# Two more row tiles transposed by DMA in a sandwich layer on eight cores

## The chip, the cores and the metric

The kernel runs on all eight cores of one Trainium2 chip. Each core takes half the rows of one of four batches (2048 of 4096 rows) and needs nothing from the others. The metric is the device time of the slowest core in microseconds. A core has TensorE for matmuls, VectorE (DVE), ScalarE (ACT), GpSimd (POOL), and a sync engine (SP) that issues DMAs. DMAs issued by GpSimd go through queue q0 (software), those issued by SP through queue q1 (hardware), and both are carried out by the same 16 DMA engines.

## The reference

```
def _L0_attn_ref(x, W_qkv, W_out):
    B, S, H = (8, 2048, 1024)
    scale = 1.0 / np.sqrt(h).astype(np.float32)
    y = jnp.einsum('bsh,oh->bso', x, W_qkv).reshape(*x.shape, 3)
    q, k, v = (y[..., 0], y[..., 1], y[..., 2])
    scores = jnp.einsum('bqh,bkh->bqk', q, k) * scale
    attn = jax.nn.softmax(scores, axis=-1)
    ctx = jnp.einsum('bqk,bkh->bqh', attn, v)
    return jnp.einsum('bsh,oh->bso', ctx, W_out)
...
x = x + _layernorm(_L0_attn_ref(_layernorm(x), W_qkv, W_out))
x = x + _layernorm(_L0_ffn_ref(_layernorm(x), router_w, w1, b1, w2, b2))
```

x has the shape (4, 4096, 1024). The feed-forward part is two matmuls with 4096 hidden units and a gelu between them, scaled by the sum of a router's two normalised weights. All matmuls run in bfloat16 with sums in float32.

## The kernel before, in words

A core holds the normalised rows of its whole batch in on-chip memory: 32 tiles of 128 rows (`xn`), of which tiles 0 to 15 are its own query rows (from `xo`) and 16 to 31 the other half (from `xr`). They are also needed transposed (`xnT`), with the 1024 features on the partitions, as the keys and as the operand from which q' is made.

The work up to the first scores goes like this:

- **The product of the query and key weights** (`am`, bfloat16, L116 `wkb,wqb`), so that the scores are x am x'.
- **q' in four groups of four row tiles** (`g` = 0 to 3). A group has eight blocks (`j`), one for each 128 output features; a block is eight matmuls of 512 columns (four tiles of 128 rows) that add up in one PSUM bank (`q_part`), and a copy by ScalarE to `qst` (`q_out`, L466). The banks rotate over six (`next_free`). Group 0 is cut up finely since its tiles come in late. `store_q` writes a group to memory, and `load_q` reads single tiles (`qt`) back; `store_q(0)`, `load_q(0)` and `load_q(1)` come ahead of groups 2 and 3 in the program.
- **The product of the value and output weights** (`bm`, L116 `wob,wvb`), 128 matmuls.
- **The scores, the softmax and the context** for 16 query tiles, and then the feed-forward part.

Each row tile is loaded by GpSimd's queue with a cast to bfloat16 (`fetch_x`). All tiles from 16 on are asked for in one go once `am` is done, behind the value and output weights (`wvb`, `wob`). VectorE takes a tile's statistics (`stats_x`), ScalarE forms the reciprocal of the deviation (`rsa`), and VectorE normalises the tile in place (`apply_x`, L294). From tile 12 on two tiles go together.

A tile is then transposed in one of two ways, and the constant `NTP` says in which. Below `NTP` it is `transpose_x`: eight 128x128 transposes on TensorE (L120) into bank 6 or 7 and a copy by ScalarE into `xnT` (L327). From `NTP` on `apply_x` itself issues one DMA transpose on the sync queue (L112), right behind the normalisation:

```
            if t >= NTP:
                t_xT[t] = DT(keys(t), xt, [t_ln[t]])
```

Every engine runs its instructions in the order in which the program puts them. The program is written out by hand in that order: a call of `norm_next` or `transpose_x` between two blocks fixes the place. Waits are on semaphores; the first matmul of a `q_part` waits for the transposed tiles that it reads and, where it opens a bank, for the copy that frees it. SP's semaphores are a ring of 16, so a DMA also waits for the one 16 issues earlier.

Of the kernel before, what the change touches and what calls it, by code (L numbers as in the profile page):

```python
# [14 lines left out]
HC = 8  # L15
# [4 lines left out]
NKT = 32  # L20
FF = 4096
NFC = 32
NTP = 16

ENGINES = ("sync", "gpsimd", "vector", "scalar", "tensor")
SEM_OF = {"vector": "vS", "scalar": "sS", "tensor": "tS", "gpsimd": "gS"}
# [53 lines left out]
def build_program():  # L80
# [33 lines left out]
    def MM(o, l, m, first, last, after=(), sig=False):  # L114
        return Q.put("tensor", lambda e, o=o, l=l, m=m, f=first, s=last:
                     e.matmul(o, l, m, start=f, stop=s), after, sig)  # L116
# [131 lines left out]
    def keys(t):  # L248

        return xnT[:, t * H:(t + 1) * H].rearrange("p (c k) -> p c k", c=HC)  # L250

    def keys4(t, c, n=4):

        return xnT[:, t * H:(t + n) * H].rearrange(
            "p (t c k) -> p c t k", t=n, c=HC)[:, c]
# [32 lines left out]
    def apply_x(u):  # L288
# [3 lines left out]
        for t in units[u]:  # L292
# [3 lines left out]
                [a])  # L296
            if t >= NTP:
                t_xT[t] = DT(keys(t), xt, [t_ln[t]])
# [5 lines left out]
    def norm_apply():  # L304
        if applied[0] < units_done[0]:
            apply_x(applied[0])
            applied[0] += 1

    def norm_next():
        u = units_done[0]  # L310
        stats_x(u)
        if applied[0] < u:
            norm_apply()
        units_done[0] += 1
# [4 lines left out]
    def transpose_x(t):  # L319
        b = 6 + t % 2  # L320
        for j in range(HC):
            tok = TP(tbank[b][:, j * 128:(j + 1) * 128],
                     xn[:, t * H + j * 128:t * H + (j + 1) * 128],
                     [t_ln[t], t_id, free[b]] if j == 0 else (), j == HC - 1)
        dst = keys(t)
        src = tbank[b].rearrange("p (c t) -> p c t", c=HC)
        t_xT[t] = free[b] = A(lambda e: e.copy(dst, src), [tok])  # L327
# [104 lines left out]
    def load_q(i):  # L432
        t_qt[i] = DS(qt[i % 2][:, :], qs[i],
                     [t_qs[i], t_s.get((i - 2, 3))])
# [5 lines left out]
    def next_free():  # L440
        b = rot[0] % 6
        rot[0] += 1
        return b

    def q_part(g, j, b, t0, n):

        for i in range(HC):
            aft = []
            if i == 0:
                aft = t_xT[4 * g + t0:4 * g + t0 + n]  # L450
                if t0 == 0:
                    aft.append(free[b])
            if g == 0 and t0 == 0 and j % 4 == 0:
                aft.append(t_am[j // 4][i])
            tok = MM(bank[b][:, t0 * 128:(t0 + n) * 128],
                     am[:, i * H + j * 128:i * H + (j + 1) * 128],
                     keys4(4 * g + t0, i, n),
                     i == 0, i == HC - 1, aft, i == HC - 1)
        return tok

    def q_out(g, j, b, tok, toks):
        o = qst[g % 3][:, :].rearrange("p (k j t) -> p k j t", k=4,
                                       j=HC)[:, :, j]
        s = bank[b].rearrange("p (k t) -> p k t", k=4)
        war = t_qs[4 * (g - 3)] if g >= 3 else None
        free[b] = A(lambda e: e.copy(o, s), [tok, war])  # L466
        toks.append(free[b])
# [3 lines left out]
    def store_q(g):  # L471
        d = DS(qs[4 * g:4 * g + 4].rearrange("k p f -> p k f"),
               qst[g % 3][:, :].rearrange("p (k f) -> p k f", k=4), t_qo[g])
        for k in range(4):
            t_qs[4 * g + k] = d
# [20 lines left out]
    for g in range(NQG):  # L496
        toks = []
        if g == 0:
            first = [(4, 0), (5, 1), (6, 3), (7, 2), (0, 4), (1, 5)]
            for j, b in first[:2]:  # L500
                q_part(0, j, b, 0, 1)
            transpose_x(1)
            for j, b in first[2:4]:
                q_part(0, j, b, 0, 1)
            norm_next()
            norm_next()
            norm_apply()
            for j, b in first[:4]:
                q_part(0, j, b, 1, 1)
            q_part(0, 0, 4, 0, 2)  # L510
            transpose_x(2)
            q_part(0, 1, 5, 0, 2)
            transpose_x(3)
            norm_next()
            for j, b in first:
                q_part(0, j, b, 2, 1)
            norm_next()
            done = []
            for n, (j, b) in enumerate(first):
                done.append((j, b, q_part(0, j, b, 3, 1)))  # L520
                if n == 1:
                    q_out(0, *done[0], toks)
                    q_out(0, *done[1], toks)
                    norm_next()
                    transpose_x(4)
            norm_next()
            transpose_x(5)
            for d in done[2:4]:
                q_out(0, *d, toks)
            done.append((2, 0, q_part(0, 2, 0, 0, 4)))  # L530
            transpose_x(6)
            norm_next()
            q_part(0, 3, 1, 0, 2)
            transpose_x(7)
            done.append((3, 1, q_part(0, 3, 1, 2, 2)))
            for d in done[4:]:
                q_out(0, *d, toks)
            norm_next()
            rot[0] = 2
        if g == 2:  # L540
            norm_apply()
        for j in range(HC if g else 0):
            if j in norm_at.get(g, ()):
                norm_next()
            b = next_free()
            q_out(g, j, b, q_part(g, j, b, 0, 4), toks)
            if g < 3 and j in (0, 2, 4, 6):
                transpose_x(4 * (g + 1) + j // 2)
        t_qo.append(toks)
        if g == 0:  # L550
            store_q(0)
        if g == 1:
            load_q(0)
            load_q(1)
# [575 lines left out]
```

How the kernel before makes its waits and increments, by code:

```python
            def body(e, items=self.items[eng]):  # L66
                seen = {}
                for after, fn, name, inc in items:
                    for s, v in after:
                        if v > seen.get(s, 0):
                            e.wait_ge(sems[s], v)
                            seen[s] = v
                    ins = fn(e)
                    if name is not None:
                        ins.then_inc(sems[name], inc)
```

## Time and profile before

| | us |
|---|---|
| median of 3 runs (1086.77 to 1164.91) | 1087.37 |
| the profiled execution | 1087.49 |
| its span on the slowest core (core 5) | 1085.9 |
| spans of the eight cores | 1084.3 to 1085.9 |
| mean granted TensorE clock | 0.997 to 0.998 |
| TensorE busy | 1064.1 (98%) |
| VectorE, ScalarE, GpSimd busy | 350.4, 315.1, 101.9 |

The span goes from the first to the last instruction; the time of an execution is 1.6 us more. All times below are counted from the start of the span of core 5. The run at 1164.91 lies apart from the other two. Busy times of different engines overlap, so they don't add up.

### The profile page before, as it was taken

The page shows a single profiled execution, that of the slowest core. Times are in us where ns is not written, and L with a number is a line of the kernel's source. Part 1 is how long each engine was busy: PE and PEld are TensorE (multiplying, and loading weights), DVE is VectorE, ACT ScalarE, POOL GpSimd, SP SyncE. Part 2 cuts the span into 40 slices and gives each one's busy share as a digit, 9 for nine tenths or more (in the row PEclk, how much of TensorE's full clock was granted, in tenths as well). Part 3 has the DMA queues.
Part 4 walks back from the last instruction along what each step waited for, and adds up shares of the span by engine and source line. Part 5 has one row for each costly group of instructions (what it writes and reads, how often), then busy time and mean ns, then how long its engine had stood idle before and what let it go on. Part 6 is the DMA issues. An engine that isn't in the chain of part 4 may idle for free.

```text
span 1085.9 us, 14321 instructions; the slowest of 8 cores (1084.3 to 1085.9 us)
## 1 busy us (share of the span) xinstructions
PE 1064.1 (98%) x5288; PEld 495.7 (46%) x5288; DVE 350.4 (32%) x723; ACT 315.1 (29%) x516; POOL 101.9 (9%) x175
## 2 busy tenths in 40 slices
PE   5999999999999999999999999999999999999996
PEld 2654444444444444444444444444444444444444
DVE  0673842333433333334332322006103300330033
ACT  1474432323332223233322323203520242023300
POOL 7430000000000000000000320001000000000000
PEclk9999999999999999999999999999999999999999
DMA  8999994443244444433349999985202220220012
GB/s 121 161 183 172 173 225 85 107 101 83 80 78 96 98 107 107 98 83 80 80 88 150 166 165 195 162 161 115 80 1 78 75 43 1 70 73 13 1 46 71
DMA packets 154980, 110.57 MB, mean 102 GB/s; under 512 B 119712, under 2 KB 130208, under 8 KB 154912
## 3 DMA queue, kind: packets, MB, share of 16 engines
q0 software_dynamic: 31120, 62.94, 29.4%
q1 hardware_dynamic: 123792, 46.72, 22.1%
q8 instruction: 43, 0.70, 0.3%
q14 instruction: 25, 0.20, 0.1%
HBM read 88.69 MB, written 25.17 MB: 105 GB/s over the span
## 4 chain that ended last, share of the span: by engine, by line
PE 94%; DMA 2%; DVE 1%; POOL 1%; issue 1%; ACT 1%; POOLq 0%; DVEq 0%; ACTq 0%
PE pAll L116 94%; DMA xn<-xo 2%; POOL wkb L110 1%; PE pAll L120 0%; POOL wqb L110 0%; ACT xnT L327 0%; DVE st L277 0%; DVE st L279 0%; DVE am L389 0%; ACT qst L466 0%; DVE yt L978 0%; ACT rsa L284 0%; DVE nma L290 0%; POOLq L1079 0%; DVE xn L294 0%
## 5 line engine op out<-in xcount | busy, mean ns | idle before, releaser
L116 PE MATMUL pAll<-xnT,qt 128*128 128x512 bf16 x1024 | 225.1, 379 | 0.0
L116 PE MATMUL pAll<-xn,pT 128*128 128x512 bf16 x1024 | 223.6, 379 | 0.0
L116 PE MATMUL pAll<-x2T,w1b 128*128 128x512 bf16 x1024 | 222.6, 379 | 0.0
L116 PEld LDWEIGHTS pAll<-xnT,qt 128*128 128x128 bf16 x1024 | 100.2, 98 | 120.8 <-issue 0.5
L116 PEld LDWEIGHTS pAll<-xn,pT 128*128 128x128 bf16 x1024 | 100.2, 98 | 120.8
L116 PEld LDWEIGHTS pAll<-x2T,w1b 128*128 128x128 bf16 x1024 | 99.8, 98 | 120.0 <-issue 0.6
L597 DVE TENSOR_REDUCE nmx<-pAll 128x1 f32<-128x1024 f32 x64 | 78.0, 1222 | 177.0 <-PE pAll L116 177.0
L603 ACT ACTIVATE pb<-pAll,nmx 128x1024 bf16<-128x1024 f32 x64 | 71.3, 1114 | 167.6 <-DVE nmx L597 167.5
L116 PE MATMUL pAll<-w2b,h1a 128*128 128x512 bf16 (+1 forms) x528 | 113.2, 373 | 0.2 <-issue 0.2
L116 PE MATMUL pAll<-w2b,h1b 128*128 128x512 bf16 (+1 forms) x528 | 113.0, 373 | 0.0
L974 ACT ACTIVATE x2r<-x2r,nm 128x1024 f32<-128x1024 f32 x15 | 17.2, 1147 | 214.4 <-DVE nm L972 214.4
L116 PEld LDWEIGHTS pAll<-w2b,h1a 128*128 128x128 bf16 x528 | 51.6, 98 | 59.5 <-issue 0.6
L116 PEld LDWEIGHTS pAll<-w2b,h1b 128*128 128x128 bf16 x528 | 51.6, 98 | 58.9
L945 DVE TENSOR_TENSOR yt<-pAll,b2b 128x1024 f32<-128x1024 f32 (+2 forms) x18 | 19.9, 1104 | 180.7 <-PE pAll L116 180.7
L841 ACT ACTIVATE h1b<-pAll,b1f 128x512 bf16<-128x512 f32 x64 | 43.2, 687 | 60.0 <-PE pAll L116 59.9
L116 PE MATMUL pAll<-xnT,am 128*128 128x512 bf16 (+2 forms) x392 | 58.5, 305 | 0.7 <-ACT xnT L327 0.7
L116 PE MATMUL pAll<-bm,uT 128*128 128x512 bf16 x256 | 57.9, 379 | 0.0
L841 ACT ACTIVATE h1a<-pAll,b1f 128x512 bf16<-128x512 f32 x64 | 42.8, 685 | 50.1 <-PE pAll L116 50.1
L658 ACT CAST ub<-pAll 128x1024 bf16<-128x1024 f32 x16 | 16.2, 1012 | 119.5 <-PE pAll L116 119.5
L116 PE MATMUL pAll<-wkb,wqb 128*128 128x512 bf16 x128 | 30.0, 394 | 12.2 <-DMA wkb<-wk 12.0
L116 PEld LDWEIGHTS pAll<-xnT,am 128*128 128x128 bf16 x392 | 31.2, 98 | 22.9 <-issue 1.1
L110 POOL DMA_DIRECT2D x2s<-xf x16 | 8.7, 545 | 345.6 <-DVE xf L719 345.6
(91 smaller groups left out, 601.1 us busy)
## 6 DMA issues: line engine op xcount, KB each, us to landing
xf<-xo POOLq DMA_DIRECT2D x16, 512.0 KB, 4.6
x2s<-xf POOLq DMA_DIRECT2D x16, 512.0 KB, 2.9
w1b<-w POOLq DMA_DIRECT2D x8, 1024.0 KB, 22.4
w2b<-w POOLq DMA_DIRECT2D x8, 1024.0 KB, 60.1
x2r<-x2s POOLq DMA_DIRECT2D x16, 512.0 KB, 4.7
y<-yt SPq DMA_DIRECT2D x15, 512.0 KB, 2.7
xn<-xo POOLq DMA_DIRECT2D x16, 256.0 KB, 30.4
xn<-xr POOLq DMA_DIRECT2D x16, 256.0 KB, 49.7
```

The costliest lines, as they stand in the source:

```text
L110: "gpsimd", lambda e, o=o, i=i: e.dma_start(o, i), after)
L116: e.matmul(o, l, m, start=f, stop=s), after, sig)
L597: mx = V(lambda e: e.tensor_reduce(n, pair[pr], AX, ALU.max, negate=True), [tok, t_cf.get(i - 2)])
L603: lambda e: e.activation(o, pair[pr], AF.Exp, bias=n, accum_out=l),
L658: t_ub[i] = A(lambda e: e.copy(o, pair[2]), [t_ctx[i], t_uT.get(i - 2), t_qs[NQT - 1]])
L841: lambda e: e.activation(o, bank[b], AF.Gelu_apprx_tanh, bias=b1f[:, fc:fc + 1]),
L945: a = V(lambda e, c=c, acc=acc: e.tensor_tensor(o[:, c], acc, b2b[:, c], ALU.add), [done, t_b2] + war)
L974: a = A(lambda e: e.activation(x[:, :], x[:, :], AF.Identity, bias=n_), [t_n, t_x2r[t]])
```

## The change

`NTP` goes from 16 to 14: tiles 14 and 15 are no longer transposed on TensorE but by DMA. Group 3 of q' reads tiles 12 to 15. Its first three blocks are formed in two halves: first the columns of tiles 12 and 13 for all three, in three banks, then those of tiles 14 and 15. The other five blocks stay whole.

```
-NTP = 16
+NTP = 14
...
         if g == 2:
             norm_apply()
-        for j in range(HC if g else 0):
+        if g == 3:
+            three = [next_free() for j in range(3)]
+            for j, b in enumerate(three):
+                q_part(g, j, b, 0, 2)
+            for j, b in enumerate(three):
+                q_out(g, j, b, q_part(g, j, b, 2, 2), toks)
+        for j in range({0: HC, 3: 3}.get(g, 0), HC):
             if j in norm_at.get(g, ()):
                 norm_next()
             b = next_free()
             q_out(g, j, b, q_part(g, j, b, 0, 4), toks)
-            if g < 3 and j in (0, 2, 4, 6):
+            if g < 3 and j in (0, 2, 4, 6) and 4 * g + 4 + j // 2 < NTP:
                 transpose_x(4 * (g + 1) + j // 2)
```

On TensorE, from the middle of group 2 to the end of group 3 (`xnT,am` are blocks of q', `ident,xn` the transposes of a tile, `wob,wvb` the product that follows):

```order
 L116 MATMUL pAll<-xnT,am 128x512 x16
 L120 MATMUL pAll<-ident,xn 128x128 x8
-L116 MATMUL pAll<-xnT,am 128x512 x16
-L120 MATMUL pAll<-ident,xn 128x128 x8
-L116 MATMUL pAll<-xnT,am 128x512 x16
-L120 MATMUL pAll<-ident,xn 128x128 x8
-L116 MATMUL pAll<-xnT,am 128x512 x72
+L116 MATMUL pAll<-xnT,am 128x512 x40
+L116 MATMUL pAll<-xnT,am 128x256 x48
+L116 MATMUL pAll<-xnT,am 128x512 x40
 L116 MATMUL pAll<-wob,wvb 128x512 x128
```

Two groups of eight transposes are gone, and 24 matmuls of 512 columns have become 48 of 256.

On the sync queue, from the two loads of `qt` to the stores of the other groups:

```order
 L108 DMA qt_69<-qs 128x1024
 L108 DMA qt_70<-qs 128x1024
-L112 DMA_TRANSPOSE xnT<-xn 128x8x128 x16
+L112 DMA_TRANSPOSE xnT<-xn 128x8x128 x18
 L108 DMA qs<-qst_53 128x4x1024
 L108 DMA qs<-qst_54 128x4x1024
```

The two new transposes stand directly behind the loads of `qt` and ahead of the 16 of the other half's tiles.

## Rows read from the trace of the kernel before

**Rows 1.** The page: busy time and share of the span; the chain that ended last.

```profile
PE 1064.1 (98%) x5288; PEld 495.7 (46%) x5288; DVE 350.4 (32%) x723; ACT 315.1 (29%) x516; POOL 101.9 (9%) x175
...
PE 94%; DMA 2%; DVE 1%; POOL 1%; issue 1%; ACT 1%; POOLq 0%; DVEq 0%; ACTq 0%
```

**Rows 2.** Timeline of TensorE: start, length, operation, count.

```profile
49.16 1.04 PE L116 MATMUL pAll<-xnT,am 128*128 128x256 bf16 x8
50.03 0.61 PE L120 MATMUL pAll<-ident,xn 128*128 128x128 bf16 x8
...
90.93 0.61 PE L120 MATMUL pAll<-ident,xn 128*128 128x128 bf16 x8
91.37 15.70 PE L116 MATMUL pAll<-xnT,am 128*128 128x512 bf16 x72
106.91 5.34 PE L116 MATMUL pAll<-wob,wvb 128*128 128x512 bf16 x24
```

**Rows 3.** Timelines of VectorE and ScalarE: tiles 14 and 15 normalised, tile 15 copied.

```profile
77.94 1.00 DVE L294 TENSOR_SCALAR xn<-xn,rsa,nma 128x1024 bf16<-128x1024 bf16 x2
...
91.66 1.02 ACT L327 COPY xnT<-pAll 128x1024 bf16<-128x1024 bf16 x1
```

**Rows 4.** Timelines of the two queues: loads of qt, last load of the other half.

```profile
79.12 0.95 SPq L108 DMA_DIRECT2D qt<-qs  x2
...
62.35 0.53 POOL L110 DMA_DIRECT2D xn<-xr  x1 [0.72 <-DMA xn<-xo]
```

**Rows 5.** Tile xnT from 104 to 109 on SP (issue in ns); page, all 16.

```profile
L112 SPq DMA_TRANSPOSE xnT<-xn x2: 1798/5278/8758, 105.8 to 107.7; - x2
...
DMA to landing us min/median/max: 13.3/13.8/14.3
...
xnT<-xn SPq DMA_TRANSPOSE x16, 4.0
```

**Rows 6.** Stretches: length, busy PE, PEld, DVE, ACT, POOL; clock, DMA share, GB/s.

```profile
90.00:104.00 14.00, 14.00 (x73) 6.62 (x71) 5.87 (x12) 5.34 (x10) 0.00 (x0) 1.00 1.07 165
104.00:114.00 10.00, 10.00 (x48) 4.51 (x46) 7.67 (x17) 4.42 (x12) 0.00 (x0) 1.00 1.08 173
```

**Rows 7.** DMA queues (packets, MB, share) in 79:90, 84:88, 110:113, 120:121.

```profile
q1 hardware_dynamic: 288, 0.52, 17.7%
...
q0 software_dynamic: 203, 0.39, 73.9%
q1 hardware_dynamic: 202, 0.38, 36.3%
...
q0 software_dynamic: 241, 0.44, 96.6%
q1 hardware_dynamic: 198, 0.05, 12.2%
...
q1 hardware_dynamic: 1136, 0.28, 128.0%
```

**Rows 8.** DMA queues 638 to 653, and the transpose issued at 636.8, w2 loading.

```profile
q1 hardware_dynamic: 1056, 0.26, 17.6%
...
uT<-ub SPq DMA_TRANSPOSE x1, 15.1
```

**Rows 9.** TensorE's first and last matmuls, then stretches as in rows 6.

```profile
9.62 7.10 PE L116 MATMUL pAll<-wkb,wqb 128*128 128x512 bf16 x24 [9.62 <-DMA wkb<-wk]
...
1075.72 1.91 PE L116 MATMUL pAll<-w2b,h1b 128*128 128x256 bf16 x16
...
1080.00:1082.00 2.00, 0.00 (x0) 0.00 (x0) 1.67 (x5) 0.00 (x0) 0.20 (x1) 0.82 0.00 0
1082.00:1084.00 2.00, 0.00 (x0) 0.00 (x0) 0.25 (x1) 0.00 (x0) 0.00 (x0) 0.50 0.75 262
```

## The prediction

> **What bounds the kernel now.** I read the page's busy shares first: TensorE is busy 98% of a 1085.9 us span, and the chain that ended last is 94% TensorE [rows 1]. So there is no slack on TensorE: work taken from it is gained in full, and any time it waits is lost in full, unless it would have waited later anyway. The profiled execution took 1087.49 us, 1.6 more than its span and 0.1 above the median of the runs shown (1087.37), so I sum against 1087.5 and compare with the median. Next I read the timeline of TensorE around the edit, to get the time at which each tile is needed [rows 2]; then VectorE and the sync queue, to get the time at which a transpose by DMA can be issued [rows 3, 4]; and last the DMA traffic there, since that decides how long it takes [rows 5 to 8].
>
> **Part 1, what leaves TensorE.** Two groups of eight 128x128 transposes go. The last one starts at 90.93 and the next matmul at 91.37 [rows 2], so each holds TensorE for 0.44 us: 2 x 0.44 = 0.9 us gained. Their two copies on ScalarE go too (1.02 us each [rows 3]). ScalarE is busy only 5.34 of 14 us there [rows 6], so that is worth nothing on the path.
>
> **Part 2, the halves.** Three blocks of 8 matmuls with 512 columns become 48 with 256 columns. A step of 512 columns is (106.91 - 91.37)/72 = 0.216 us [rows 2], one of 256 columns (50.03 - 49.16)/8 = 0.109 us [rows 2]: 24 x 0.216 = 5.2 against 48 x 0.109 = 5.2 us. The cost is nothing. ScalarE gets three results 0.9 us apart instead of 1.7 us; TensorE wants their banks again only three blocks later, and ScalarE has the time [rows 6]: also nothing.
>
> **Part 3, when the second halves start.** The stretch of 72 matmuls that begins at 91.37 is the last block of q' group 2 (8 x 0.216 = 1.7 us) and then group 3. Without the two transposes group 3 begins at 91.4 + 1.7 - 0.9 = 92.2. The three first halves need only tiles 12 and 13 and take 24 x 0.109 = 2.6 us. At 94.8 TensorE needs tiles 14 and 15, both.
>
> **Part 4, when the two transposes can be issued.** Tiles 14 and 15 are normalised by 78.9 (two operations that start at 77.94 and take 1.00 [rows 3]). On the sync queue they stand behind the two loads of qt, which are issued at 79.12 and end at 80.07 [rows 4]. The first such transpose before took 1.8 us to issue, its follower started 1.9 us later [rows 5]. So they are issued at about 80.1 and 82.0, which leaves 14.7 and 12.8 us.
>
> **Part 5, how long they take.** This is the term that decides. With empty queues a transpose of this size lands 4.0 us after issue in the median [rows 5], and then the edit would work. But the queues aren't empty. The 16 loads of the other half's rows were all issued by 62.9 [rows 4] and keep the DMA engines at a share of 1.07 to 1.08 until 114 [rows 6]; the first pair of transposes, issued into that backlog at 105.8 and 107.7, took 14.3 and 13.3 us [rows 5] and landed together at 120.1 and 121.0. The packets say why. While q0 (the loads) and q1 (the sync queue) both have work, they are served one for one: 203 to 202 in four microseconds at 84 to 88 [rows 7], 241 to 198 in three at 110 to 113, where q1's were a transpose's small packets [rows 7]. Once the loads are gone q1 alone moves 1136 in one microsecond [rows 7]. A transpose of one tile has 1056 packets [rows 8]. So it waits its turn 1056 times behind packets of the loads, which are some seven times as large (0.44 MB in 241 against 0.05 MB in 198 [rows 7]).
>
> By the Trainium skill (DMA: Bandwidth & Descriptors, Queues, rings and completion order) each engine takes turns between the queues it has work for, at the granularity of a packet. The trace agrees, with 203 packets to 202.
>
> Rate: a q0 packet costs 0.966 x 3 us x 16 / 241 = 192 ns of an engine, a q1 packet 0.122 x 48 / 198 = 30 ns [rows 7]. A turn of both is 222 ns, less the 9% by which the shares there exceed 1: 204 ns, or 16 / 0.204 = 78 turns a microsecond. The observed rates are 66 to 80. Two transposes need 2 x 1056 = 2112 turns, that is 27 us at 78 and 32 us at 66. They begin when the qt loads, ahead of them in the same queue, are done: all 288 of their packets lie before 90 [rows 7]. So tile 15 lands at 117 to 122. Does the backlog last that long? Before, q0 has nothing left in the microsecond from 120 [rows 7]; the new packets add 2112 x 30 ns / 16 = 4 us to it. At 90 us up to 30 us of loads at 80 packets a microsecond [rows 7] are ahead, 2400 packets, more than the 2112 turns. So it does last, and it also caps the wait at about 124. I take 118, near the low end, since the higher rate stands in windows where both queues are full.
>
> Bounds from the nearest rows: if each transpose lands as one alone does in the backlog of the w2 loads, 15.1 us after issue [rows 8], tile 15 lands at 97; if only when the lengthened backlog has drained, at 124.
>
> **Sum.** Stall 118 - 94.8 = 23.2 us. Nobody makes it good: behind the waiting matmul in TensorE's queue stand the rest of the group, the product of the value and output weights, and all scores; ScalarE's copies and the statistics of tiles 16 and 17 hang behind them and move along. Then the clock. TensorE's granted clock fell to 0.82 and then 0.50 (1.2 GHz) in the stretches that begin 2.4 and 4.4 us after its last matmul, which began its group at 1075.72 and was over by 1077.6 [rows 9]; 23 us idle will do the same. What it costs to come back is seen at the start of the program, where TensorE also begins after a long wait: the first 24 matmuls of 512 columns take 7.10 us [rows 9], where 24 x 0.216 and 0.2 for the end of the last make 5.4. That is 1.7 us. Total: 1087.5 - 0.9 + 23.2 + 1.7 = 1111.5, say 1111: 2.2% over the median. Later stages gain nothing back: the 16 transposes that follow would now be free of the backlog, but TensorE didn't wait for them before.
>
> **Rivals.**
> (a) Forecast, tile 15 lands at 115 to 122: 1108 to 1115. For it: the one-for-one packet counts in two windows with two packet sizes. Against: no row has two transposes wholly inside the backlog. Chance 0.72.
> (b) Not slower: the transposes arrive in time. Their place is 94.8, the start of the second halves. If the time after issue is some 14 us however long the backlog (as the rows of the first pair read by themselves), tiles 14 and 15 land at 80.1 + 14.3 = 94.4 and 82.0 + 13.3 = 95.3, the stall is 0.5 us and the time 1087.5 - 0.9 + 0.5 = 1087.1. It decides at 14.7 us from the issue of the first. Against: both of that pair landed within 1 us of each other and just as the loads ran out. Chance 0.13. The Trainium skill (DMA: Bandwidth & Descriptors, Latency and other measured facts) gives a DMA transpose an effective 261 GB/s; an estimate by it is 2 us for both tiles, which would bring them in time too, but the 15.1 us of one tile in a backlog [rows 8] speaks against using it here.
> (c) In between: the transposes get about two packets a turn, or both are served side by side, and tile 15 lands at 97 to 109: 1090 to 1102. Chance 0.10.
> (d) It lands only when the backlog is gone on the slowest DMA engine, 124: a stall of 29.2, 1117.5. Chance 0.05.
>
> **Numbers.** Some 2% (22 us here) is what a measurement of this kernel can tell from no change. The bound is at 1087.4 x 1.02 = 1109.1, which is a landing at 115.6. Of (a) I put seven eighths above it, of (d) all: slower 0.68. Faster by 2% is impossible, since only 0.9 us is removed: 0.01. The rest, 0.31, is within 2%. Likeliest case: 1111. The range runs from 1097, inside (c), to 1118, above (d), and leaves out (b) and part of (c).
>
> **What would show it.** Right: in the changed profile one gap in TensorE of about 23 us near 95, released by a DMA into xnT; the first two transposes issued near 80 and 82 and landing near 104 and 118; q0 and q1 packets one for one from 90 to 117; the first matmuls behind the gap at about twice 0.109 us a step; from there everything displaced by about 24 us. Wrong, towards (b): no gap over 1 us, and landings 13 to 15 us after issue. Wrong in size: if the slowest DMA engine lags, the gap is longer; if the clock is not lowered, 1.7 us less. The forecast as a whole fails if transposes aren't served in turn with the loads over a whole stretch, since all of part 5 rests on 3 and 4 us windows.

## The result, and the profile after

The changed kernel takes 1108.74 us (median of 4 runs, 1108.00 to 1109.34) against 1087.25 for the kernel before: a ratio of 1.0198, with a 95% interval of 1.0184 to 1.0212. It is slower by 21.5 us, where 23.5 were forecast (1111). The profiled execution took 1109.23 us, its slowest core is now core 1 with a span of 1107.7 us; core 1 had 1085.7 before.

Some executions of the kernel before and of e2, e4 and e8 below ran with one die at a lower clock; they are left out of the medians, ratios and intervals given here.

The page of the changed kernel answers to [rows 1]:

```profile
PE 1066.7 (96%) x5296; PEld 498.6 (45%) x5296; DVE 350.2 (32%) x723; ACT 313.1 (28%) x514; POOL 101.8 (9%) x175
...
PE 91%; DMA 5%; DVE 1%; ACT 1%; issue 1%; SPq 0%; POOL 0%; POOLq 0%; DVEq 0%; ACTq 0%
PE pAll L116 91%; DMA xnT<-xn 3%; DMA qs<-qst 1%; DMA wkb<-wk 1%; SPq L112 0%; ACT qst L466 0%; ACT xnT L327 0%; POOL wqb L110 0%; DVE st L277 0%; DVE st L279 0%; POOL wkb L110 0%; PE pAll L120 0%; DVE am L389 0%; DVE yt L984 0%; SPq L108 0%
```

TensorE's share of the span falls from 98% to 96%, and "DMA xnT<-xn" is new on the chain that ended last, with 3% of the span. The timeline of TensorE in the changed kernel (start, length, count, idle before and who ended it) shows the place, beside [rows 2]:

```profile
83.70 10.34 PE L116 MATMUL pAll<-xnT,am 128*128 128x512 bf16 x59
114.82 14.08 PE L116 MATMUL pAll<-xnT,am 128*128 128x256 bf16 x64 [20.78 <-DMA xnT<-xn]
128.74 27.79 PE L116 MATMUL pAll<-wob,wvb 128*128 128x512 bf16 x128
```

The view begins at 84, inside the first row's stretch. TensorE finishes the three first halves at 94.04 and then stands still for 20.78 us, until a transpose by DMA lands. There is one such gap and no other; on the other seven cores it is 18.9 to 20.8 us long. The same query on the sync queue for the tile xnT, first from 79 to 81.5 and then from 75 to 120, beside [rows 5]:

```profile
L112 SPq DMA_TRANSPOSE xnT<-xn x1: 4058/4058/4058, 79.6 to 79.6; - x1
DMA to landing us min/median/max: 21.8/21.8/21.8
...
L112 SPq DMA_TRANSPOSE xnT<-xn x2: 4058/8406/12754, 79.6 to 83.7; - x2
DMA to landing us min/median/max: 21.8/26.4/31.0
```

The first transpose was issued at 79.6 and landed 21.8 us later, at 101.4. The second was issued at 83.7 and landed 31.0 later, at 114.7, where TensorE goes on. Neither is anywhere near the 13.3 and 14.3 us of the pair before. The packets of the two queues in the changed kernel, from 90 to 104, from 104 to 110, from 110 to 114 and from 114 to 117, beside [rows 7]:

```profile
q0 software_dynamic: 1244, 2.27, 95.5%
q1 hardware_dynamic: 1241, 0.31, 17.2%
...
q0 software_dynamic: 518, 0.94, 93.6%
q1 hardware_dynamic: 521, 0.13, 17.2%
...
q0 software_dynamic: 326, 0.59, 100.2%
q1 hardware_dynamic: 218, 0.05, 11.9%
...
q0 software_dynamic: 364, 0.42, 82.8%
q1 hardware_dynamic: 3, 0.00, 0.2%
```

1244 to 1241, then 518 to 521: one for one over 20 us. In the last four microseconds the transposes run out: of their 218 packets only 3 come after 113. After 114 they are done but for 3 more packets, while q0 still has 364 to move, so they finished before the backlog did. Last, stretches of the changed kernel (columns as in rows 6) show the clock:

```profile
94.00:96.00 2.00, 0.04 (x1) 0.00 (x0) 1.85 (x5) 0.00 (x0) 0.00 (x0) 1.00 1.13 205
96.00:98.00 2.00, 0.00 (x0) 0.00 (x0) 1.90 (x4) 0.00 (x0) 0.00 (x0) 0.60 1.13 201
98.00:100.00 2.00, 0.00 (x0) 0.00 (x0) 1.78 (x5) 0.00 (x0) 0.00 (x0) 0.50 1.14 184
...
118.00:120.00 2.00, 2.00 (x11) 1.45 (x10) 0.00 (x0) 0.59 (x1) 0.00 (x0) 0.50 0.00 0
120.00:122.00 2.00, 2.00 (x10) 0.83 (x9) 0.00 (x0) 0.59 (x1) 0.00 (x0) 0.92 0.00 0
```

The granted clock is down to 0.50 (1.2 GHz) in the stretch from 98, and full again only within the one from 120, over 5 us after the matmuls resumed.

### The profile page after: what moved, and what is told of

It is laid out like the page before. It is cut to its first block, busy times and chain, and to the rows that moved or that the text cites. A ratio compares the mean times of both kernels' runs of the same rounds, so it can differ in the third digit from the quotient of the medians.

```text
span 1107.7 us, 14343 instructions; the slowest of 8 cores (1105.2 to 1107.7 us)
## 1 busy us (share of the span) xinstructions
PE 1066.7 (96%) x5296; PEld 498.6 (45%) x5296; DVE 350.2 (32%) x723; ACT 313.1 (28%) x514; POOL 101.8 (9%) x175
## 4 chain that ended last, share of the span: by engine, by line
PE 91%; DMA 5%; DVE 1%; ACT 1%; issue 1%; SPq 0%; POOL 0%; POOLq 0%; DVEq 0%; ACTq 0%
PE pAll L116 91%; DMA xnT<-xn 3%; DMA qs<-qst 1%; DMA wkb<-wk 1%; SPq L112 0%; ACT qst L466 0%; ACT xnT L327 0%; POOL wqb L110 0%; DVE st L277 0%; DVE st L279 0%; POOL wkb L110 0%; PE pAll L120 0%; DVE am L389 0%; DVE yt L984 0%; SPq L108 0%
## 5 line engine op out<-in xcount | busy, mean ns | idle before, releaser
L116 PE MATMUL pAll<-xnT,am 128*128 128x512 bf16 (+2 forms) x416 | 61.1, 306 | 21.5 <-DMA xnT<-xn 20.8
L116 PEld LDWEIGHTS pAll<-xnT,am 128*128 128x128 bf16 x416 | 34.9, 101 | 43.5 <-issue 22.4
```

## The experiments

Theory A is the prediction's: while the loads of GpSimd's queue have work, every packet of a transpose waits for one of theirs. The rivals are that the transposes take that long in this stage by themselves, whatever else moves (B), or that the DMA engines share out bytes or time, not packets (C). In e1 and e2 the question is whether the halves have a price.

**e1, whole blocks.** The halves are taken out of the changed kernel.

```
-            three = [next_free() for j in range(3)]
-            ... first and second halves of three blocks
...
-        for j in range({0: HC, 3: 3}.get(g, 0), HC):
+        for j in range(HC if g else 0):
```

> The changed kernel without the two halves: all eight blocks of q' group 3 are whole, tiles 14 and 15 still go by DMA. Theory A (the two transposes land when they have had their turns among the loads' packets, whatever TensorE does): tile 15 lands near 114 us as in the changed kernel, TensorE stops 2.6 us earlier, at about 91.5, so the gap is about 23.4 us instead of 20.8 and the time about 1108.7 + 2.6 = 1111.3. Theory B (the halves themselves cost something, so that the changed kernel's loss is partly theirs): 1108.7 or less.

1110.93 us (2 runs). On its slowest core the gap is 22.84 us, from 90.84 to 113.68: it begins earlier and ends about where it did. By the medians the halves hide 2.2 us (1110.93 - 1108.74). The intervals of the two ratios overlap slightly (1.0198 to 1.0239 here), but the executions themselves lie apart (1110.59 and 1111.26 against 1109.34 at most).

**e2, halves alone.** In the changed kernel:

```
-NTP = 14
+NTP = 16
```

> The halves alone: tiles 14 and 15 are transposed on TensorE as before, and the first three blocks of group 3 are formed in two halves. Theory A (48 steps of 0.109 us cost what 24 of 0.216 do): 1087.3, ratio 1.000 within 0.001, no gap in TensorE near 95. Theory B (the halves cost something): above 1088.5.

1086.88 and 1086.76 us beside 1087.23 for the kernel before on the same chip: the halves cost nothing that can be seen. Two executions are too few to show that they gain a few tenths.

**e3, one tile.** In the changed kernel:

```
-NTP = 14
+NTP = 15
```

> Only tile 15 goes by DMA, tile 14 stays on TensorE; halves kept. Theory A (1056 turns at 88 a microsecond, from about 89 us on): it lands near 101.5, TensorE has a gap of some 6.6 us, the clock falls and costs some 2.4: 1087.3 - 0.4 + 6.6 + 2.4 = 1095.9. Theory B (a transpose takes as long as the backlog lasts, however few there are): it lands near 114 again, gap near 19, time near 1108.

1096.59 us, 95% interval of the ratio 1.0066 to 1.0107. Timeline of TensorE in e3, and the packets from 90 to 101:

```profile
102.78 13.56 PE L116 MATMUL pAll<-xnT,am 128*128 128x256 bf16 x64 [7.96 <-DMA xnT<-xn]
...
q0 software_dynamic: 953, 1.74, 93.8%
q1 hardware_dynamic: 953, 0.24, 18.0%
```

953 to 953. With half of the transposes' packets the landing is 12 us earlier, at 102.6 (issued at 80.1, 22.5 us), as A has it. By itself this doesn't tell A from B, since tile 14 also took 21.8 us in the changed kernel; it excludes only that a transpose waits for the whole backlog.

**e4, transposes first.** `load_q(0)` and `load_q(1)` go from behind group 1 to behind the normalisation of tiles 14 and 15:

```
-        if g == 1:
-            load_q(0)
-            load_q(1)
         if g == 2:
             norm_apply()
+            load_q(0)
+            load_q(1)
```

> The changed kernel with the two loads of qt moved behind the two transposes on the sync queue. Theory A (turns, and the qt loads' 288 packets are served ahead of the transposes in the same queue): the transposes' packets begin near 83 instead of 89, tile 15 lands near 107.5, gap near 13.5 us: 1108.7 - 7 = 1101.7. Theory B (the time from issue to landing in this stage is set by the transposes themselves, 22 and 31 us): they are issued about 1 us earlier, time near 1107.7.

1103.68 us (one execution). The transposes were issued at 78.2 and 79.9, the gap is 14.55 us instead of 20.78 and ends at 109.14. From 90 to 100 the packets are 862 to 861. The two landed 19.2 and 29.1 us after issue, and the first was issued in 1.61 us instead of 4.06. The second landed at 109.0, 5.7 us earlier than in the changed kernel, though it was issued only 3.8 earlier. By 90 the two had had 524 turns here, against 129 in the changed kernel, where the 288 packets of the qt loads stood ahead of them. The time is 2 us over A's and 4 under B's; one execution leans to A and doesn't decide.

**e5, smaller packets of the loads.** Each load of the other half's tiles is cut in two:

```
+        t_x.append([DG(xn[:, t * H + h:t * H + h + 512],
+                       src[row:row + 128, h:h + 512], after)
+                    for h in (0, 512)])
```

> The changed kernel with each of the 16 loads of the other half's tiles cut into two of 512 columns, so that its packets are of 1024 bytes instead of 2048 and twice as many. Theory A (one packet of the sync queue for one of the loads): behind 1024-byte packets there are some 130 turns a microsecond instead of 88 once the weights' loads (2048 bytes) are over near 93; tile 15 lands near 89 + 4 + (2112 - 350)/130 = 107, gap near 13, time near 1101.5. Theory C (the DMA engines share out bytes or time, not packets): no change, 1108.7.

1101.02 us (1.0102 to 1.0143), against 1101.5 by A and 1108.7 by C. The gap is 11.08 us, where A had 13. Packets from 94 to 104, and TensorE:

```profile
q0 software_dynamic: 1538, 1.40, 90.3%
q1 hardware_dynamic: 1535, 0.38, 34.3%
...
106.23 14.05 PE L116 MATMUL pAll<-xnT,am 128*128 128x256 bf16 x64 [11.08 <-DMA xnT<-xn]
```

The loads are the same bytes in twice as many packets, and the transposes get 153 turns a microsecond instead of 89. This is the run that tells A from C: what is dealt out in turn is packets.

**e6, loads held back.** In the changed kernel the 16 loads of the other half's tiles are issued behind the normalisation of tile 15, and the first of them waits for its transpose, with the others behind it in the same queue:

```
+            for t in range(16, NKT):
+                fetch_x(t, [t_xT[15]] + t_am[0] if t == 16 else ())
```

> The changed kernel with the 16 loads of the other half's tiles held back until both transposes have landed. The loads of the value and output weights stay as they are and are over near 93. Theory A (turns): until 94 the transposes get some 400 turns, then q1 is alone at some 1000 packets a microsecond and tile 15 lands near 96.5; the gap is some 2 us and too short for the clock to fall: 1087.3 - 0.9 + 2 = 1088.4, range 1086.5 to 1091. Theory B (the transposes take 22 and 31 us from issue by themselves): 1108.7.

1093.26 us (4 runs, 1090.02 to 1093.37; ratio 1.0027 to 1.0061). At the place in question it went as A says. TensorE in e6, xnT on the sync queue, and the packets from 90 to 93:

```profile
94.72 11.41 PE L116 MATMUL pAll<-xnT,am 128*128 128x256 bf16 x64 [0.96 <-DMA xnT<-xn]
...
DMA to landing us min/median/max: 10.1/11.9/13.7
...
q1 hardware_dynamic: 787, 0.19, 135.8%
q0 software_dynamic: 19, 0.03, 5.5%
```

The same two transposes, issued at 80.1 and 84.5, now land in 13.7 and 10.1 us instead of 21.8 and 31.0, and once q0 has run out q1 is alone. B falls. But the time is 5 us over the forecast and outside its range, since a new gap opened 79 us further on:

```profile
173.41 15.66 PE L116 MATMUL pAll<-xn,pT 128*128 128x512 bf16 x64 [5.11 <-DMA pT<-pb]
```

**e7, both.** e6 with the qt loads behind the transposes as in e4.

> As e6, and the two loads of qt stand behind the transposes on the sync queue. Theory A: the transposes take turns from near 83 to 94, get some 950 of their 2112, and are done near 95.5; gap 0 to 1.5 us: 1087.3 - 0.9 + 1 = 1087.4, range 1086.3 to 1089. Theory B: 1107.7.

1091.55 us (10 runs, 1087.89 to 1094.10; 1.0019 to 1.0047), outside the expected range. The gap near 94 is gone altogether: both transposes land 13.5 to 14.1 us after issue, in time. The gap for pT stays, 5.58 us near 172 on the slowest core; on two of the eight cores there is none, and in the others it is 0.3 to 5.2 us. In e7 that transpose (issued at 156.1) took 15.9 us to land; before, on core 5, the first two took 6.8 to 7.7. What had moved was the three loads of xf. They wait for the last stores of q', which had ended later with everything behind the held loads, so they were issued at 156.55 instead of 152.10. The timelines of the two queues in e7:

```profile
156.07 17.28 SPq L112 DMA_TRANSPOSE pT<-pb  x2
...
156.55 1.58 POOL L110 DMA_DIRECT2D xf<-xo  x3 [53.44 <-DMA qs<-qst]
```

**e8, the xf loads later too.** `load_x(0)` to `load_x(2)` are called behind the transpose of the first pT instead of ahead of it, and wait for it.

```
...
-                     [t_x2s.get(i - 3), t_xnb.get(i - 3), t_qs[4], t_qs[8]])
+                     [t_x2s.get(i - 3), t_xnb.get(i - 3), t_qs[4], t_qs[8],
+                       t_pT.get(0)])
...
```

> e7, and the first three loads of xf (512 KB each, wanted only near 199 us) wait until the first transposed softmax tile pT has landed. In e7 they were issued 0.5 us after that transpose and TensorE then waited 5.6 us for it near 172. Theory A (the same turns of one packet for one between a transpose and loads): pT lands some 7 us after issue instead of 15.9, the gap near 172 goes, and what stays is the 0.9 us taken from TensorE: 1087.0 - 0.9 = 1086.1, range 1085.7 to 1087.0. Theory B (pT is late because the stores of q' ahead of it in its own queue ended later): the gap stays, near 1091.

1087.73 us (7 runs), ratio 1.0004 (0.9993 to 1.0014): no difference from the kernel before, and outside the expected range. On all eight cores pT now lands 6.7 to 7.3 us after issue (10.3 to 15.9 in e7) and its gap is gone, so the xf loads were the cause, and holding loads back helps a second transpose too. That one packet for one was at work there isn't shown by it. The expected 0.9 us doesn't appear. The first pT on the sync queue of core 4, the slowest, and TensorE there, which now waits for the last tiles of xnT:

```profile
DMA to landing us min/median/max: 6.7/6.7/6.7
...
94.48 11.41 PE L116 MATMUL pAll<-xnT,am 128*128 128x256 bf16 x64 [0.17 <-DMA xnT<-xn]
...
148.66 20.88 PE L116 MATMUL pAll<-xnT,qt 128*128 128x512 bf16 x96 [1.33 <-DMA xnT<-xn]
```

Together 1.5 us, more than was saved. The last transpose of that series was issued at 145.2 in e8 and at 138.2 before: the held loads took up the slack that these tiles had.

**e9, four tiles.** e8 with `NTP = 12`, and the last loads of `wvb` and `wob` held as well.

> e8 with four tiles by DMA (12 to 15) and the last two loads of the value and output weights held back as well until tile 15 has landed, so that the loads' packets run out near 85 us. Theory A: the four transposes get some 450 turns until then and go alone afterwards, all land by 91, no gap near 92; TensorE has 4 x 0.44 = 1.8 us less: 1085.3, if the other half's tiles, now some 4 us later, don't hold up the scores; range 1084.8 to 1088. Theory B (the transposes don't get faster when the loads are out of the way): a gap of over 5 us, above 1092.

1090.46 us (7 runs; 1.0019 to 1.0040), outside the range. No gap near 92, as A says; but the wait for the last tiles of xnT has grown to 3.34 us and the clock is low behind it. TensorE in e9, and a stretch (columns as in rows 6, the granted clock third from the end):

```profile
149.06 22.54 PE L116 MATMUL pAll<-xnT,qt 128*128 128x512 bf16 x96 [3.34 <-DMA xnT<-xn]
...
149.00:151.00 2.00, 1.94 (x5) 0.74 (x6) 0.00 (x0) 0.00 (x0) 0.00 (x0) 0.51 1.04 356
```

96 matmuls take 22.54 us here and 20.88 in e8: 1.7 us more. The two make 5.0 us, against 1.8 us taken off TensorE.

## Why the prediction was right, point by point

- **Gain of 0.9 us, parts 1 and 2.** Right as far as it can be seen: e2 shows no cost of the halves (1086.8 against 1087.2). The 0.9 us itself is smaller than any interval here and was never seen alone.
- **Need at 94.8, part 3.** TensorE stopped at 94.04 on core 1. The forecast was made from core 5 of another execution. There the transposes of tile 12 on TensorE began at 79.23; in the changed kernel, on core 1, they began at 78.28, and nothing ahead of them was edited. So most of the 0.8 us is the difference between two executions and not an error of the sum.
- **Issue at 80.1 and 82.0, part 4.** 79.6 and 83.7. The first took 4.06 us to issue and not 1.8, as the qt loads still stood in the queue (in e4, without them, it took 1.61). The landings were set by the turns and not by this.
- **Duration, part 5.** The mechanism was right, and only its rate was off. The mis-sized term is "16 / 0.204 = 78 turns a microsecond": from 90 to 104 there were 1241 / 14 = 89. A q0 packet cost 0.955 x 224 / 1244 = 172 ns of an engine and not 192, and the shares summed to 1.13 and not to 1.09. 2112 turns at 89 are 24 us instead of 27. Tile 15 landed at 114.7, 3.3 us before 118, and the rate is most of that. The rest is small and partly cancels: 129 turns had been taken by 90, where the sum began; 118 was chosen 1 us above its own 117; and nearly all packets were over by 113, 1.7 us ahead of the landing, for which the sum had no term. The rate had been read from the three microseconds from 110 to 113 before, ahead of which q1 had moved one packet in two microseconds, so it was read from the start of a transpose. That it came out low for this reason isn't shown. All 2112 packets are found: 129 by 90 (417 of q1 less the 288 of qt), then 1241, 521, 218 and 3.
- **Gap 23.2 us.** 20.8: the landing came 3.3 us earlier than forecast, and TensorE stopped 0.8 us earlier.
- **Clock 1.7 us.** It cost 2.7: from 114.82 to 128.74 TensorE did 24 steps of 256 and 40 of 512 columns, which take 24 x 0.109 + 40 x 0.216 = 11.3 us at the full clock and took 13.9. The low level lasted over 5 us after the restart, while at the start of the program the loss was only 1.7. Over the eight cores the same 64 matmuls took 12.95 to 14.08 us, against 11.41 in e6, so the cost is 1.5 to 2.7 us and the slowest core had the most.
- **Sum.** -0.9 + 20.8 + 2.7 = 22.6 us beside 22.0 between the spans of core 1. Later stages gave back 0.6 us at most, where nothing was forecast. That the total came out 2.3 us off is in part luck: the gap was 2.4 us too long, the clock 1.0 us too cheap, and the two errors have opposite signs.
- **Rival (b)**, the fixed 14 us, is excluded by the changed kernel's own rows and by e6. Rival (c), two packets a turn, by 1244 to 1241; and (d), a landing only when the backlog is gone, by the 364 packets that q0 still had after 114. The prediction gave 0.68 to a loss of over 2%; the measured loss is 1.98%, with 1.84 to 2.12% as its interval, and leaves that open.

My expectations for e6 to e9 failed in one and the same way: each edit removed the gap that it aimed at, and I gave no price to what the held loads would push further on. What moved in e7 is shown by e8; in e8 and e9 it is read from the gaps and not tested by a run. The last transpose of xnT was issued 7.0 us later in e8 than before. The traces show where most of this arose: the first of the series was issued at 110.7 instead of 105.8, as its tile was normalised that much later, and issuing the second kept the sync queue for 11.56 us instead of 8.76, with the other 14 behind it. So a second price of a backlog is the time for which it keeps the sync queue.

## What to carry to other kernels

Beside the loads measured here, with packets of 1024 and 2048 bytes, a DMA transpose cost turns, not bytes: count its packets (1056 for a tile of 128 x 1024 in bfloat16), and divide by the turns that a window of this stage shows (153 and 89 a microsecond). Beside packets of 4096 bytes the count did not hold (below). An unloaded landing time (4 us here) says nothing in a stage where a long queue of loads is waiting; look at the queue's packets in that very stage. And where the loads are held back for it, check every later user of both queues, since the slack that they had is what pays: the three loads of xf in e7, the last tiles of xnT in e8 and e9.

## What the runs showed of the hardware that was not expected

- The ratio of turns holds to a few packets in a thousand over 10 to 14 us (1244 to 1241, 953 to 953, 1538 to 1535), for transposes behind loads with packets of 2048 and of 1024 bytes. It does not hold beside the xf loads of e7, whose packets are twice as large again (4096 bytes): from 160 to 164 there were 758 packets of q1 to 91 of q0, and pT was late all the same. The three loads have 432 packets in all and the transpose of a pT over 4000, so only a few of its packets can each have waited for one of theirs. By an estimate from the trace the loads took 6.9 us of the 16 engines (43.4% of the time from 156 to 172), which would be most of the 9.2 us by which pT landed later than in e8. No run tests this, and how the engines divide their time there stays open.
- Issuing the second transpose kept the sync queue busy for 12.75 us; for the second of the series before, tile 17, it was 8.76. Nothing stood behind it here, but in e8 the rest of the series did.
- After 20.8 us without a matmul the granted clock took more than 5 us of matmuls to come back, and behind a wait of 3.34 us in e9 it was 0.51 from 149 to 151. Behind the wait of 1.33 us in e8 the same 96 matmuls took 20.88 us, as long as at the full clock.
